# Key weight tiles loaded over two DMA queues, the first in halves; the bias columns turned behind four context tiles; two stores held until the last shift row has landed

## The reference

```python
Q = (query @ Wq.T + bq)...; K = (key @ Wk.T + bk)...; V = (value @ Wv.T + bv)...   # 16 heads of 32
attn = jax.nn.softmax(scores, axis=-1)
expert = jnp.einsum('bsd,eod->ebso', out, We) + be[:, None, None, :]
expert = expert.mean(axis=0)
return expert @ Wo.T + bo
...
x = x + jnp.tanh(g_xattn[0]) * _L0_xattn_ref(_layernorm(x, axis=-1), ctx_1024, ctx_1024, ...)
x = x + jnp.tanh(g_ffn[0]) * _L0_ffn_ref(_layernorm(x, axis=-1), w_gate, w_expert, b_expert)
```

## Time and profile before

| | us |
|---|---|
| median of 3 runs | 408.39 (408.34 to 409.35) |
| the profiled execution, device time | 408.48 |
| its span in the profile | 406.7 |
| TensorE busy in the span | 400.1 (98%) |
| VectorE busy | 336.5 (83%) |
| ScalarE busy | 228.2 (56%) |
| GpSimd busy | 167.0 (41%) |

### The profile page before, as it was taken

How to read it: one execution, slowest core, us unless ns; L and a number is a source line. 1 busy time by engine, 2 the same in 40 slices (tenths; PEclk the granted TensorE clock), 3 DMA queues, 4 the chain that set the end, 5 groups by cost and what they waited for, 6 DMA issues and landing times.

```text
span 406.7 us, 8772 instructions
## 1 busy us (share of the span) xinstructions
PE 400.1 (98%) x3126; PEld 190.6 (47%) x3126; DVE 336.5 (83%) x683; ACT 228.2 (56%) x320; POOL 167.0 (41%) x154
## 2 busy tenths in 40 slices
PE   8999999999999999999999999999999999999996
PEld 4556664444444444444444444444444444454444
DVE  6549566986897989988998999899897688779996
ACT  4435423678556764946585485748556473876110
POOL 2027999224171157309034530803261063460371
PEclk9999999999999999999999999999999999999999
DMA  7999991464058408814860683286059016241585
GB/s 266 319 388 396 366 382 39 104 126 148 2 129 194 158 12 168 233 68 98 145 236 2 149 228 106 65 175 240 0 131 238 9 33 172 79 135 27 96 167 185
DMA packets 65517, 63.19 MB, mean 155 GB/s; under 512 B 41765, under 2 KB 45233, under 8 KB 65475
## 3 DMA queue, kind: packets, MB, share of 16 engines
q1 hardware_dynamic: 60363, 56.19, 50.7%
q0 software_dynamic: 1632, 3.49, 3.2%
q10 hardware_dynamic: 3480, 2.96, 2.2%
HBM read 29.59 MB, written 12.98 MB: 105 GB/s over the span
## 4 chain that ended last, share of the span: by engine, by line
PE 93%; DVE 2%; ACT 1%; DMA 1%; issue 1%; SPq 0%; POOL 0%; ACTq 0%; DVEq 0%
PE ps L840 76%; PE ps L456 9%; PE ps L588 3%; PE ps L405 2%; DMA ctx_raw<-in_ctx_dram 1%; ACT probs L1237 1%; ACT mixT_hi L397 0%; SPq L729 0%; PE ps L1164 0%; DVE xb L1570 0%; DVE wqT_lo L1680 0%; DVE mixT_lo L398 0%; POOL known L1931 0%; PE ps L606 0%; PE ps L525 0%
## 5 line engine op out<-in xcount | busy, mean ns | idle before, releaser
L1237 ACT ACTIVATE probs<-ps 120x1024 f32<-120x1024 f32 x64 | 62.0, 1024 | 21.8 <-PE ps L840 21.7
L1604 DVE TENSOR_REDUCE neg_max<-ps 128x16 bf16<-128x1920 f32 x32 | 68.6, 2143 | 3.7 <-PE ps L840 3.7
L1990 POOL TENSOR_TENSOR attn_lo<-attn,attn_hi 128x512 f16<-128x512 f32 x28 | 31.8, 1158 | 91.3 <-ACT attn_hi L1237 91.3
L840 PE MATMUL ps<-xnT_hi,wqT_hi 128*128 128x512 f16 x128 | 48.6, 380 | 0.0
L840 PE MATMUL ps<-mixT_hi,attn_hi 128*128 128x512 f16 x128 | 48.6, 380 | 0.0
L840 PE MATMUL ps<-mixT_lo,attn_hi 128*128 128x512 f16 x128 | 48.5, 379 | 0.0
L840 PE MATMUL ps<-xnT_lo,wqT_hi 128*128 128x512 f16 x128 | 48.5, 379 | 0.0
L1998 POOL TENSOR_TENSOR xb<-xb,mix_bias 128x512 f32<-128x512 f32 x32 | 39.6, 1270 | 15.1 <-DVE cb_col L1547 15.1
L1237 ACT ACTIVATE q_hi<-ps,bias_cols 128x512 f16<-128x512 f32 x32 | 22.1, 689 | 31.5 <-PE ps L840 31.5
L840 PE MATMUL ps<-q_stack,k_stack 97*120 97x512 f16 x128 | 35.0, 390 | 1.2 <-DMA q_stack<-shift 0.7
L840 PE MATMUL ps<-probs,den_sel 120*32 120x256 f32 x512 | 34.1, 384 | 0.0
(11 more groups left out here) (277 smaller groups left out, 807.0 us busy)
## 6 DMA issues: line engine op xcount, KB each, us to landing
xb<-in_x_dram SPq DMA_DIRECT2D x8, 1024.0 KB, 7.0
q_stack<-q_hi SPq DMA_DIRECT2D x48, 128.0 KB, 2.4
out_dram<-xb SPq DMA_DIRECT2D x6, 1024.0 KB, 6.7
raw<-in_L_xattn_We_dram SPq DMA_DIRECT2D x5, 1024.0 KB, 11.2
q_stack<-q_lo SPq DMA_DIRECT2D x32, 128.0 KB, 2.6
xb<-in_L_xattn_We_dram SPq DMA_DIRECT2D x3, 1024.0 KB, 10.1
k_stack<-k_scratch SPq DMA_DIRECT2D x8, 360.0 KB, 4.4
k_scratch<-k_hi ACTq DMA_DIRECT2D x16, 120.0 KB, 7.2
```

Of the source, the lines that this page charges most:

```text
L840: return e.matmul(out_, a, b, start=start, stop=stop, **kw)
L1237: return e.activation(out_, in_, func, **kw)
L1604: e.tensor_reduce(neg_max[:, :, :, g], quad[:, :, 0:NT * SK].rearrange("p j (t s) -> p t j s", t=NT), AX.X, ALU.max, negate=True).then_inc ...
L1990: e.tensor_tensor(attn_lo[:, g, :], attn[:, g, :], attn_hi[:, g, :], ALU.subtract).then_inc(s_alo, 1)
```

## The change

Four edits. The key weight tile 0 is loaded as two column halves, one from SP and one from ACT, and tile 2 goes from SP to ACT, both ahead of ACT's bias rows; the first unit waits for both halves. The unit "bias" moves from behind the key weight to behind four context tiles. The first of SP's stores of batch 6 waits for the last shift row.

```diff
-                unit((name, i), pe, consts + [(s_wt[name][i], 16)], **evac)
+                unit((name, i), pe, consts + [(s_wt[name][i], 32 if (name, i) == ("wkT", 0) else 16)], **evac)
...
         weight_units("wkT", pair=(wkT_hi, wkT_lo), scale=QK_SCALE)
+        for t in range(HALF):
+            ctx_unit(t)
         unit("bias", turn(lambda i: bias_rows[:, :], 1, 3 * NK, P), consts + [(s_bqk, 16 * 3)],
              dve=lambda e, b: e.tensor_tensor(bias_cols[:, :], b[:, 0:3 * NK], bias_unit[:, :], ALU.mult))
-        for t in range(HALF + 1):
-            ctx_unit(t)
+        ctx_unit(HALF)
         k_units(0, [lambda t=t: ctx_unit(t) for t in range(HALF + 1, CT)])
...
-            load_tiles("wkT", Wk)
+            load(slots[slot_of["wkT"]][:, 0, 0:D // 2], Wk[0:P, 0:D // 2], s_wt["wkT"][0])
+            load_tiles("wkT", Wk, (1, 3))
...
                     if r == B - 2:
+                        e.wait_ge(s_rsh, 16 * B)
                         store_tiles(r, (0, 1))
...
+            wk_slot = slots[slot_of["wkT"]]
+            e.dma_start(wk_slot[:, 0, D // 2:D], Wk[0:P, D // 2:D]).then_inc(s_wt["wkT"][0], 16)
+            e.dma_start(wk_slot[:, 2, :], Wk[2 * P:3 * P, :]).then_inc(s_wt["wkT"][2], 16)
             for i, b_ in enumerate((bq, bk, bo)):
```

More of the change, by code:

```diff
@@ L732, in w_view, with load_tiles @@
                 return w.rearrange("(t p) d -> p t d", p=P)
-            def load_tiles(n, w):
-                for i in range(NK):
+            def load_tiles(n, w, tiles=range(NK)):
+                for i in tiles:
                     load(slots[slot_of[n]][:, i, :], w[i * P:(i + 1) * P, :], s_wt[n][i])
-            load_tiles("wkT", Wk)
+            load(slots[slot_of["wkT"]][:, 0, 0:D // 2], Wk[0:P, 0:D // 2], s_wt["wkT"][0])
+            load_tiles("wkT", Wk, (1, 3))
             for t in range(CT):
```

## The result

| | us, median | runs | ratio, 95% interval |
|---|---|---|---|
| before | 408.14 (407.27 to 409.35) | 22 | |
| changed | 408.86 (408.39 to 410.49) | 22 | 1.0018 (1.0010 to 1.0025) |
| changed, once more with the last experiments | 408.69 (408.44 to 409.01) | 11 | 1.0014 (1.0005 to 1.0023) |

The change made the kernel 0.7 us slower (0.4 to 1.0 by the interval); 408.9 and a loss of 0.5 were forecast.

The account below looks back on a forecast made before the run. TensorE was taken as the bound, busy 400.1 of 406.7 us. +0.7 (bias columns), -0.15 to 0.2 (landings) and 0 (stores) made +0.5 on 408.48, thus 409.0, lowered by 0.1 to 408.9; range 407.8 to 409.8.

Parts of the forecast that it names:

- Part 1: At the first key product: bias columns, written by DVE behind four contexts, delay it from 11.58 to about 12.3, +0.7 us.
- The chain of low parts: On DVE before the first key product: the fifth low part would begin at 12.05, with bias columns done at 12.2.
- Part 2: At the opening key weight loads: two queues make tiles and contexts land earlier, worth 0.15 to 0.2 us.
- upper bound of 0.48: At the opening loads: context 0 is issued about 0.48 us earlier, the whole saving if issue is all that counts.
- rival C: At the opening loads: tile 1 lands late through sharing with tile 2, giving 409.6 us and more; chance 0.11.
- the 5.9 from which it was to cost: At tile 1's landing: sharing costs nothing up to 5.9 us and one for one beyond.
- The formula for that, landing + 6.3: On DVE before the first key product: bias columns are done 6.3 us after tile 1's landing, 12.2 for 5.9.
- Part 3: At the last batch's shift row near 345 us: holding stores shortens TensorE's 0.69 us wait, but 0 reaches the end.
- The signs: In the profile after, for example: first key product at 12.0 to 12.4, context 0 at 7.6 to 8.0.
- a product before 11.6: At the first key product: a start this early would show the forecast wrong, with landings moved far more.
- B: At the opening loads: two queues make landings 0.5 to 1.2 us earlier, giving 407.9 to 408.6 us; chance 0.24.
- D: At the last batch's shift row: the stall at 345 us does reach the end, 0.69 us more gain; chance 0.07.

## Why the prediction was right

**Part 1, the bias unit (+0.7 forecast).** Right in mechanism and about a quarter too small: alone it costs 0.9 us. The chain of low parts ends where I put it: with context 0 landing at 7.7, the bias columns began at 11.84 (I had 12.05, with a start of the chain 0.14 later). The term that was mis-sized is the step from the bias columns to the matmul: I allowed 0.1 for signal and weight load, and the four profiles show 0.57. The signal and the weight load were not the fault; the weight load begins 0.03 us ahead of the matmul. Left out were the five waits of the product's list that TensorE's sequencer takes one by one, 0.1 us each, once the bias columns are there.

**Part 2, the loads (-0.15 to -0.2 forecast).** This is the step that was mis-sized: alone it is worth 0.65 to 0.9 us, beyond the upper bound of 0.48 that I gave to earlier issue. I argued that 1.3 MB have to pass in any case. They do, but the engines had been passing them more slowly than they can: 225 GB/s between 4 and 5 us. The same window in the changed kernel:

```profile
4.00:5.00 1.00, 1.00 (x5) 0.61 (x4) 0.61 (x8) 0.33 (x2) 0.00 (x0) 1.00 1.01 305
```

One microsecond is a poor witness, though: the next one in this profile has only 199. From 3 to 7 us together, the kernel before and the run with the loads alone:

```profile
3.00:7.00 4.00, 3.34 (x19) 2.25 (x18) 2.84 (x16) 1.78 (x4) 0.50 (x5) 1.00 0.96 307
```

```profile
3.00:7.00 4.00, 3.91 (x22) 2.88 (x20) 2.57 (x16) 2.87 (x4) 0.50 (x5) 1.00 1.04 382
```

The four profiles with the loads of before have 266 to 324 GB/s there, the eight with the new loads 319 (the changed kernel's first) to 389.

The rule of the Trainium skill, page "DMA: Bandwidth & Descriptors", section "Issuing engines are not separate DMA queues", that a second issuing engine saves only issue time, doesn't cover this: issue accounts for 0.55 us of about 1. The rest goes along with the higher rate; why the engines move more with these loads no run separates, and two queues alone don't do it, since the run with two tiles in halves moved 305. That two queues share fits two rows: tile 1 at 5.45 instead of 4.15 in the changed kernel (4.6 to 5.0 in the other seven profiles with these loads), tile 0 at 4.5 instead of 3.5 when it was left whole. That is rival C's mechanism; here it stayed under the 5.9 from which it was to cost.

**Together.** Added as they stand, the two parts would give a loss of 0 to 0.3 us (0.9 less 0.65 to 0.9); measured are 0.7 and, the second time, 0.6. So beside the moved bias unit the loads are worth only 0.2 to 0.4, near what I had booked for them, and not what they are worth alone. With the unit in its old place the product follows the high parts and gains all of the earlier landing. Behind four contexts it follows DVE's chain, which in the first profile starts with tile 1 (late by sharing) at 6.97 and not with context 0. The formula for that, landing + 6.3, gives 11.75 for 5.45, and 11.45 was measured. That the loss came out near is thus in part luck, and that the time did to 0.04 us is luck outright: the kernel before measured 408.14 in this comparison, 0.25 below the 408.39 that I had started from, and the loss was 0.2 above the forecast.

**Part 3, the stores (0 forecast).** The amount was right, and so was the reason: the waits for the shift row and for the group 3 scores add up to the same. Before 0.69 and none, changed 0 and 0.68, changed again 0.35 and 0.37, stores alone 0.63 and none. The distance stays within 391.95 and 392.10 in twelve of the thirteen profiles with `gate_exp` in its place, whatever the shift row did (the thirteenth, with the bias behind three, has 392.28: against the loads alone it loses 0.1 us at the scores of 160.68 and again at those of 197.18, far ahead of the shift row; why isn't known). Wrong was the belief that the held stores shorten the row's landing: it hangs on the transfer of `q_lo` ahead of it. The vanished wait in the changed kernel's profile looks like the edit at work, and isn't.

**The signs.** The first profile has the product at 12.01, at the edge of the 12.0 to 12.4 that I gave, tile 1 later and the waits in the last batch as I said. It misses three: TensorE idle for 0.90 and not 0.4 to 0.7, tile 2 turned at 6.18 and not before 6.06, context 0 at 7.2 and not 7.6 to 8.0. And the second profile shows a sign that I had called wrong, a product before 11.6 (11.54), for the reason that I gave: the landings moved far more.

**The rivals.** B, landings 0.5 to 1.2 earlier, did happen in the landings, and yet not in the sum, because I had priced it with a DVE chain that starts with context 0, while the low parts of the key weight stand ahead of it. C's sharing happened without reaching its price. D is refuted by the distances.

## What to carry to other kernels

A read-out that many wait for should be placed by the queue of the engine that does it, not by the engine that produces it: here one 0.16 us instruction behind four low parts cost 0.9 us, and two places earlier it cost nothing that could be measured. An instruction with a long list of waits also pays for the rest of the list when one near its front ends last: here 0.5 us for five, read from the traces. When several small edits go in together, a profile that shows a stall gone doesn't show which edit removed it, and a stall that is gone isn't time won: measure the distance from the first point the edits share to the end. What is needed first is the piece to split over two queues: tile 0 whole landed 1.0 later with a whole piece on the other queue. More isn't better: with tile 1 in halves too, the gain was gone.

The best version is the loads alone, 407.4 to 407.5 us: 0.65 to 0.9 us under the kernel before and about 1.3 under the changed one.

## What I hadn't expected of the hardware

- TensorE's sequencer takes semaphore waits one by one, 0.1 us each, even those long fulfilled. With five still to take, the first key matmul began 0.56 to 0.57 us after the end of the bias columns, in four profiles; with none left to take, at 353.40, it was 0.05 us after the exponential.
- With key weight tile 0 in halves on two queues and tile 2 on the second, context 0 landed 4.1 to 5.0 us after its issue; on one queue 4.8 to 5.6.
- The early transposes took up to 1.8 times as long as the later ones, for a stretch that differs from profile to profile of much the same start, while the granted clock read 1.00: four took 1.09 at 3.79 and 0.63 at 5.61 in the changed kernel, 1.06 up to 7.8 with tile 0 whole, and only 0.63 from 3.93 on with the bias behind three. The product's time in one profile holds some of this as chance; the medians are the safer witness.
